# The router of a mixture-of-experts layer taken earlier in the attention trunk, in five units instead of four

## The reference

```python
x = x + xattn0(ctx, layernorm(x), ctx)     # 16 heads of 64, causal
x = x + ffn0(layernorm(x))                 # fp4 quantised, inner width 352
x = x + xattn1(layernorm(x), ctx)          # 16 heads, keys in two segments (77 and 51)
x = x + moe(layernorm(x))                  # 8 experts, the best 2 of each token

def moe(x):                                # x: 2048 tokens x 128
    logits = silu(x @ rw1 + rb1) @ rw2 + rb2            # 128 -> 512 -> 8
    k_logits, k_index = top_k(logits, 2); k_prob = softmax(k_logits)
    out = 0
    for e in range(8):
        we = sum(where(k_index == e, k_prob, 0), -1)
        out = out + we[:, None] * (silu(x @ w1[e] + b1[e]) @ w2[e] + b2[e])   # 128 -> 512 -> 128
    return out
```

## Time and profile before

| | us |
|---|---|
| median of 3 runs | 739.5 |
| the profiled execution | 740.57 |
| its span, first to last instruction | 738.8 |
| PE busy in the span | 644.8 (87%) |
| DVE busy | 534.2 (72%) |
| ACT busy | 437.4 (59%) |
| POOL busy | 305.8 (41%) |

### The profile page before, as it was taken

The page is one execution under the profiler, slowest core; times in us unless marked ns, Lnnn a source line. Parts: engine busy times, 40 slices in busy tenths (PEclk is TensorE's granted clock), DMA queues, the critical chain, the costliest instruction groups (busy, mean ns, idle before and its releaser), DMA issues.

```text
span 738.8 us, 16537 instructions
## 1 busy us (share of the span) xinstructions
PE 644.8 (87%) x5835; PEld 588.2 (80%) x5835; DVE 534.2 (72%) x1444; ACT 437.4 (59%) x1117; POOL 305.8 (41%) x427
## 2 busy tenths in 40 slices
PE   2789999999989989999999999999999539866990
PEld 2678888888878889999999999998887539866990
DVE  7796586888888889888988968776666244533554
ACT  3568878787777765555655555567365107323760
POOL 3234344344434532534443424243364454266560
PEclk9789999999999999999999999999999659867996
DMA  9600000000000002177550500000000011111225
GB/s 230 200 1 1 3 1 1 2 1 1 3 1 1 3 15 69 48 142 129 110 108 1 144 2 2 1 1 3 1 26 19 16 38 50 37 41 51 66 55 177
DMA packets 49390, 33.27 MB, mean 45 GB/s; under 512 B 9415, under 2 KB 45869, under 8 KB 49309
## 3 DMA queue, kind: packets, MB, share of 16 engines
q1 hardware_dynamic: 47036, 27.55, 15.8%
q0 software_dynamic: 2272, 4.67, 1.9%
HBM read 17.57 MB, written 14.63 MB: 44 GB/s over the span
## 4 chain that ended last, share of the span: by engine, by line
PE 53%; DVE 15%; issue 13%; ACT 8%; POOL 5%; DMA 4%; SPq 1%; POOLq 0%; DVEq 0%; ACTq 0%
PE ps_j L386 7%; PE ps_s L535 6%; PE ps_h L610 5%; PE ps_t L574 5%; PE ps_h L589 5%; ACT scores L727 4%; PE ph L1390 4%; PE ps_j L348 4%; DVE scores L989 4%; PE py L1404 4%; PE ps_j L350 3%; PE ps_j L349 3%; DVE neg_max L996 3%; POOL xs_scratch L1318 2%; PE pf L498 2%
## 5 line engine op out<-in xcount | busy, mean ns | idle before, releaser
L1230 POOL TENSOR_TENSOR probs<-scores,rsums 128x308 f32<-128x308 f32 (+1 forms) x192 | 151.9, 805 | 228.9 <-DVE rsums L1009 228.7
L1004 DVE TENSOR_REDUCE sums<-scores 128x4 f32<-128x308 f32 (+1 forms) x192 | 90.9, 501 | 43.8 <-ACT scores L727 34.6
L574 PE MATMUL ps_t<-ident,probs 128*128 128x128 f32 x512 | 79.3, 278 | 17.5 <-ACT probsT L739 17.2
L727 ACT ACTIVATE scores<-scores,neg_max 128x128 f32<-128x128 f32 x256 | 81.6, 393 | 17.5 <-DVE neg_max L996 17.0
L739 ACT ACTIVATE probsT<-ps_t 128x512 f32<-128x512 f32 x128 | 75.4, 589 | 23.8 <-PE ps_t L574 23.8
L634 ACT ACTIVATE QT<-ps_j 128x512 f32<-128x512 f32 x64 | 38.2, 598 | 80.5 <-PE ps_j L350 80.4
L535 PE MATMUL ps_s<-KT,QT 64*128 64x128 f32 x1024 | 77.1, 292 | 0.8 <-ACT KT L640 0.8
L574 PEld LDWEIGHTS ps_t<-ident,probs 128*128 128x128 f32 x512 | 58.9, 143 | 23.3 <-issue 21.5
L589 PE MATMUL ps_h<-probsT,V 128*64 128x128 f32 x1024 | 71.4, 282 | 0.8 <-DVE x_sb L775 0.8
L535 PEld LDWEIGHTS ps_s<-KT,QT 64*128 64x128 f32 x1024 | 64.6, 194 | 9.1 <-issue 1.9
L610 PE MATMUL ps_h<-Wo,headsT 128*128 128x128 f32 x512 | 71.1, 283 | 0.2 <-ACT headsT L745 0.2
(11 more groups left out here) (236 smaller groups left out, 1620.0 us busy)
## 6 DMA issues: line engine op xcount, KB each, us to landing
xs_scratch<-xs SPq DMA_DIRECT2D x8, 1032.0 KB, 8.1
xt<-xs_scratch SPq DMA_DIRECT2D x39, 64.5 KB
w1b<-in_L_ffn_w_dram SPq DMA_DIRECT2D x1, 2048.0 KB, 9.6
big_raw<-in_L_ffn_w_dram SPq DMA_DIRECT2D x8, 256.0 KB, 4.4
ysum<-y_scratch SPq DMA_DIRECT2D x4, 512.0 KB, 5.3
x_sb<-in_x_dram SPq DMA_DIRECT2D x4, 256.0 KB, 3.6
ctx_sb<-in_ctx_dram SPq DMA_DIRECT2D x4, 256.0 KB, 4.9
Wo<-in_L_xattn_Wo_dram SPq DMA_DIRECT2D x2, 512.0 KB, 6.7
```

Source lines behind the costliest of these rows:

```text
L574: ins = nc.tensor.transpose(ps_pT[:, j * S:(j + 1) * S], probs[s % 2][:, j, :], ident[:, :])
L727: ins = nc.scalar.activation(scores[s % 4][:, j, :], scores[s % 4][:, j, :], ACT.Exp, bias=neg_max[:, s % 4, 0, j:j + 1])
L1004: ins = nc.vector.tensor_reduce(sums[:, p4, i, :], scores[p4][:, :, k0:k1], AX_X, ALU.add)
L1230: ins = nc.gpsimd.tensor_tensor(probs[(s - 1) % 2][:, :, k0:k1], scores[r][:, :, k0:k1], rsums[:, r, i, :].rearrange("p (h a) -> p h a", a ...
```

## The change

Units replace quads: `UNITS` is (0,4), (4,4), (8,4), (12,2), (14,2) in batches. Units 0, 1 and 2 start at steps 114, 117 and 120 instead of 116, 121 and 126, so that two units are in progress at a time; their list is made at step 124 instead of 131. Unit 3 (batches 12, 13) is routed in steps 128 to 131, with the tail's own silu. Unit 4 (batches 14, 15) is handled between tiles 0 and 10. The norm slots of the pairs start at other steps, pairs 3, 4, 5 and 6 earlier. The bias transposes go to step 98. Each `router_up` of units 0 to 2 now takes one bank (`pf[0]`) in four turns, half of them at the end of the step; the logits take `pf[1]`, and the totals for the list are a fourth piece of `ranks`. The sends stand at steps 118 to 127 (three in a step, then two); those of unit 3 follow the trunk. The last two trunk steps are woven with the start of the tiles: `turn(0)` stands after step 130, in bank `py[0]`, and DVE copies tile 0's weights before step 130. `late_list` is cut in three: `early_done` (tile 3), `late_tiles` (7), `late_list` (9). `RING` is 8, and there are 6 buffers `ysb`.

```diff
-RING = 6
+UNITS = [(0, QUAD), (QUAD, QUAD), (2 * QUAD, QUAD), (3 * QUAD, PAIR), (3 * QUAD + PAIR, PAIR)]
+RING = 8
+YB = 6
...
-            q, t = divmod(N - FFN_TO, 5)
-            return (q, t) if 0 <= q < EARLY_Q else (None, None)
+        D_AT = [(81, 83, 84, 85), (91, 93, 94, 95), (101, 103, 104, 105), (106, 107, 108, 109), (111, 112, 113, 114),
+                (116, 117, 118, 119), (124, 125, 126, 127), (NG * STEPS + 4,)]
+        BIAS_AT = 98
+        ROUTE_FROM = (114, 117, 120, NG * STEPS)
+        LIST_AT = ROUTE_FROM[EARLY_U - 1] + 4
+        TAIL = NG * STEPS + 2
...
+            def route_end(u, t):
+                if u < EARLY_U:
+                    if t < 2:
+                        router_up(u, 2 * t + 1)
+                    if t == 2:
+                        router_logits(u)
+                    if t == 3:
+                        ranks(u, u == EARLY_U - 1)
+                else:
+                    if t == 0:
+                        router_up(u, 2)
+                        router_up(u, 3)
+                    if t == 1:
+                        router_logits(u)
+                    if t == 2:
+                        ranks(u, False)
...
+            TWIN_AT = (110, 113, 119, 127)
+            SEND_AT = [{118: range(0, 3), 119: range(3, 6), 120: range(6, 8)},
+                       {121: range(0, 3), 122: range(3, 6), 123: range(6, 8)},
+                       {124: range(0, 2), 125: range(2, 4), 126: range(4, 6), 127: range(6, 8)}]
...
+            tail(TAIL)
             turn(0)
+            tail(TAIL + 1)
+            tail(TAIL + 2)
...
+            for N in range(TAIL, TAIL + 3):
+                tail(N)
+            for j in range(TOPK):
+                send(U - 1, 0, j)
             rstd_of(GROUPS - 1, 2, "D")
-            twin(Q)
+            for j in range(TOPK):
+                send(U - 1, 1, j)
+            twin(U)
             for i in range(NT):
-                if 11 <= i < 11 + QUAD:
-                    for j in range(TOPK):
-                        send(Q, i - 11, j)
+                if 7 <= i < 7 + PAIR * TOPK:
+                    send(U, (i - 7) // TOPK, (i - 7) % TOPK)
                 scatter(i)
...
             sp.wait_ge(MS["list"], 1)
-            sp.wait_ge(s_sent, 16 * TOPK * EARLY_Q * QUAD)
+            sp.wait_ge(s_sent, 16 * EARLY_ROWS // P)
```

More of the change, by code:

```diff
@@ L515, in step @@
+            def step(G, g, s, lay, prev, first=False, last=False, nxt=None, f=None, fd=None):
                 n = G * STEPS + s
@@ L625, in trunk_tensor @@
             pe.wait_ge(s_split0_lo, 3)
-            trunk(pe, step)
-            return turn_d, router_up, router_logits, ranks, totals
+            return trunk(pe, step), turn_d, router_up, router_logits, ranks
         def trunk_scalar(act):
@@ L762, in trunk_scalar @@
             copy_k(0, 0)
-            trunk(act, step)
-            return mean_square, high
+            return trunk(act, step), mean_square, high, router_silu
         def trunk_vector(dve):
@@ L1019, in shifted_scores, with step @@
                 ins.then_inc(SS["shifted"], 1)
-            def step(G, g, s, lay, prev, first=False, last=False, nxt=None, f=None):
+            def step(G, g, s, lay, prev, first=False, last=False, nxt=None, f=None, fd=None):
                 n = G * STEPS + s
@@ L1217, in slot, with step @@
                     rstd_of(c, 1, "C")
-                if s == 6 and d is not None:
-                    rstd_of(d, 2, "D")
-            def step(G, g, s, lay, prev, first=False, last=False, nxt=None, f=None):
+            def step(G, g, s, lay, prev, first=False, last=False, nxt=None, f=None, fd=None):
                 n = G * STEPS + s
@@ L1458, in moe_gpsimd @@
         def moe_gpsimd(pool, pieces):
-            rstd_of, twin, send = pieces
-            Q = QUADS - 1
+            tail, rstd_of, twin, send = pieces
+            U = len(UNITS) - 1
             def scatter(i):
@@ L1481, in moe_vector @@
         def moe_vector(dve, pieces):
-            slot, choose, place, late_list = pieces
+            tail, slot, choose, place, early_done, late_tiles, late_list = pieces
             chain = Chain(dve, "m_chain")
-            Q = QUADS - 1
+            U = len(UNITS) - 1
             def gate_difference():
@@ L1545, in moe_vector @@
             stage_w2(0, e)
+            for N in range(TAIL, TAIL + 3):
+                tail(N)
+            for part in (1, 2):
+                slot(5, part, d=GROUPS - 1)
             for i in range(NT):
```

501 lines of the change are left out of this document (259 added, 242 removed).

## The result

The changed kernel took 710.65 us (median of 4 runs, 708.93 to 714.26), the kernel before 739.98 beside it (738.93 to 741.65). The ratio is 0.9608, 95% interval 0.9562 to 0.9654: 29 us faster. The forecast was 700 in a range of 688 to 715. The time lies in the forecast's range; the gain is 29 us where 40 were forecast. Where a run took over 1.5% more than the fastest of its kernel, its ratio is over the other runs (experiment 2 alone has one).

A forecast was written before the change was run, and what follows sets the result against it. PE bounds the trunk; about 35 us lie in two gaps behind it. Stretches of 495.3, 81.3, 15.5, 41.4, 43.5 and 22.1 end at 699.1; plus 1.8, less 1.1 gives 699.8, called 700, range 688 to 715.

The forecast's parts named there:

- The first gap: From 570.0 to tile 0's first matmul at 609.4: early sends, landing and load leave the path; 39.4 us becomes 15.5.
- The tail: Step 128's transposes to tile 0: 8.3 us of PE work, 12 with waits, 3.5 for half clock, sum 15.5 us.
- Tiles 0 to 15: Tiles 31.2, unit 4's PE pieces 5.9, waits 1.0, 1.5 and 1.8: sum 41.4 us instead of 61.0.
- a closed second gap: In tiles 0 to 15: four late sends from tile 7, not eight from 11, and a split list; 61.0 becomes 41.4.
- Tiles 16 to 38 and the end: Later tiles take 43.5 us instead of 46.3 with more buffers; scatter, reading back and weighted sum stay 22.1.
- Steps 114 to 127: Last trunk steps gain 6.6 us: logits 3.6, ranks 0.9, half clock 1.7, totals and transpose 0.4; 74.7 becomes 81.3.
- 49 us in about 58, it fits: POOL in steps 118 to 127: 24 sends 30.5, probabilities 12.5, copies and roots some 6, within the time available.
- 1.7 us each: Trunk's last steps: each group of logits is followed by 3.4 us at clock 0.50, so the third brings 1.7 too.
- the finer weave: `router_up` of units 0 to 2 in one bank, four turns: costed at nothing, up to 1 us a turn if ACT is late.
- The rule and the rows: Skill's rule, clock closes on idleness, would make the sum 3.4 us lower; the forecast followed the trace's rows instead.
- a step 128 beyond 585 would say that the denser trunk isn't only the sum of its matmuls: Warning sign at the end of the trunk's last steps; step 128's transposes were forecast at 576.6.
- the rivals: Tail stays long 0.17; second gap half closes 0.12; even better 0.17; slower 0.02; change doesn't do what it says 0.02.

The follow-up runs named there:

- experiment 2: Changed kernel with the logits of units 0 to 2 in two groups of 16, a turn apart; 706.51 us, ratio 0.9512 to the kernel before.
- experiment 1: Changed kernel with all 24 early sends moved behind step 132 on POOL; 737.35 us (one run).
- the kernel after: The changed kernel itself, with the whole change against the kernel before; 710.65 us, ratio 0.9608.
- Experiment 7: Changed kernel with unit 4's ranks, placing, list parts and late sends one tile later; 712.22 us, ratio 0.9616 to the kernel before.
- experiment 10: Changed kernel with unit 4's pieces back at their earlier places between the tiles, sends at tiles 11 and 12; 712.41 us, ratio 0.962 to the kernel before.
- Experiment 4: Changed kernel with 6 buffers xt and 4 buffers ysb as before, instead of 8 and 6; 715.65 us, ratio 0.9656 to the kernel before.
- experiment 11: Kernel of experiment 9 with norm slots of pairs 3 and 4 partly later and gate values behind the last tile; 704.93 us, ratio 0.9512.
- experiment 5: Changed kernel with logits of units 0 to 2 summed over only 128 of 512 hidden values; 698.12 us, ratio 0.9441 to the kernel before.
- experiment 6: Changed kernel with units 0 to 2 starting at steps 114, 118, 122, list at step 126, later sends; 720.6 us, ratio 0.972 to the kernel before.
- experiment 9: Changed kernel with logits of units 0 to 2 turned round, router weights stationary and hidden values moving; 705.16 us, ratio 0.9537 to the kernel before.
- experiment 8: Changed kernel with norm slots of pairs 3 and 4 one step later in part; 709.3 us, ratio 0.9586 to the kernel before.
- experiments 3: Changed kernel with tile 0's turn, copy and weights behind the last trunk step, not woven in; 714.32 us, ratio 0.9652 to the kernel before.

## Why the forecast was right, and where it was short

**The first gap: right.** The tail was sized 4.7 us too long: 3.5 of them are the half clock, for it ran at 1.00 throughout (and half of 8.3 us of work would have cost 4.2, not 3.5), the rest are waits. The mechanism, early sends that leave only x itself on the path, is shown by experiment 1: 27.3 us come back when they go.

**Tiles 0 to 15: right, 3.2 us short, all of it waits.** PE's busy time, 36.9, is the forecast's 31.2 + 5.9. The waits are 7.7 instead of 4.3: 2.5 for `chosen`, 1.1 for `w1s`, and the rest where a part of the list stands on DVE in front of the next weights. DVE's timeline of the kernel after (answers to the earlier trace rows):

```profile
622.25 0.28 DVE L1233 TENSOR_TENSOR over<-pf,iota_m 128x128 f32<-128x128 f32 x1
...
623.60 0.17 DVE L1238 TENSOR_TENSOR tiles_e<-done_e,tiles_e 128x8 f32<-128x8 f32 x1
624.54 0.43 DVE L1558 COPY w1s<-w1b 128x516 f32 x1 [0.78 <-DVE tiles_e L1238]
```

Here one part of the list takes 1.5 us, and 0.8 pass until the engine takes the copy up, with PE's weights for `ph` waiting until 625.04. I had cut the list into parts and priced each against DVE's slack, without the gap behind each. Experiment 7 shows that moving such a piece only moves its cost. That no `px` waits over 1 us for `xt` was right. Of the two reasons that the forecast gave for a closed second gap, half as many late sends and an earlier start for them, the earlier start alone turned out to be worth little (experiment 10).

**Tiles 16 to 38 and the end: right** (44.1 for 43.5, 22.3 for 22.1). Experiment 4 gives the rings 2.2 us there; the 0.6 that the sum was short, and more, are the gate values in tile 18 (1.5 us, experiment 11), a piece of DVE that it did not name.

**Steps 114 to 127: the step that failed**, 88.0 for 81.3. The work term was right to 0.2 us, and so was POOL: "49 us in about 58, it fits", with sends of 1.04 us; experiment 1 takes them away and the stretch stays. (A send and its issue were added up as 1.26, though 1.03 and 0.3 are 1.33; nothing hangs on it.) Two terms were too small. The first is the half clock, "1.7 us each" for three groups: 8.5 us instead of 5.1 in this execution. The mechanism was the one that the forecast read from the earlier trace rows, that the clock falls behind a group of logits; experiment 5 shows it by its absence. Its size was the mistake: before, both groups were followed by 3.4 us, and I took that as the price of a group. In the profiles here the same three groups bring 13.6 to 27.3 us in 14 steps, and the rows say what goes with the length. In steps 114 to 127 of the profiles with whole groups of 32 pairs, the kernel before among them, the fall came 11 times behind the start of the group's last matmul, and every time the piece at 0.50 was 3.4 us long; both groups of the earlier trace rows are of this kind. It came 15 times inside a group, so that the rest of the logits ran at half clock, and 14 of those pieces were 6.8 to 13.7 us long (one was 3.4). In the kernel after, units 0 and 1 are of the first kind and unit 2 of the second: 1.7 + 1.7 + 5.1 is the 8.5. What decides where in a group the fall comes is not shown; a pitch of four steps did not make it better (experiment 6), and experiment 2 leaves open whether a split does. The second is the waits, 5.5 us for 2.0. I had costed the finer weave at nothing, with up to 1 us for each turn as its price if it was late; PE's waits name `hidT`, `xnT_lo` and `probs` with 4.5 us together. Taking the sends away leaves 3.8, so up to 1.7 us are POOL's; that the rest is the router's own chain in shorter turns fits the names of the waits and was not tried.

**The rule and the rows.** In the kernel after PE is busy 3.76 of 3.80 us ahead of the first fall and all the time behind it, and no wait of it in these steps is longer than 1.6 us. The Trainium skill, page "TensorE: Matmul & The Clock Gate", "Part 1: The HAM clock gate", has the clock close on idleness. By that rule steps 114 to 127 would have had none of the 8.5 us; the rows disagree, and experiment 5 says that they had them because of the logits. What these have of their own is the form: 32 pairs that load 128 x 128 weights to move 8 columns. Turned round (experiment 9) the same sums leave 6.8 us at 0.50, and none in experiment 11. No fall in either profile comes inside a group of turned logits or within 6 us behind it.

**Ahead of step 114**, 2.4 us were lost and none forecast: the forecast left the stretch up to step 114 as it was, although the change moves pieces of PE into it. The rows at experiment 8 show 1.45 us of work, 0.75 of waits and 0.2 from before step 98.

**In sum**: + 2.4 ahead, + 6.7 in the trunk, - 4.7 in the tail, + 3.2 and + 0.6 in the tiles, + 0.2 at the end, 8.4 us on 699.1. The forecast's own mark, "a step 128 beyond 585 would say that the denser trunk isn't only the sum of its matmuls", was met at 585.7. Of the rivals none is what happened: the tail is short and the second gap closed.

## What to carry to other kernels

A chain of waits that names an engine is a question: take that engine's work away from the stretch (experiment 1) before it is called the bound. Split a stretch into work, clock and waits, since kernels compared by their sum alone differ by a clock that varies more than most edits. Do not take the price of a slow piece from two cases that were alike: look at where in the work the clock fell. And on an engine that is full, matmuls that load wide weights for a few moving columns cost more than their own time; turning the operands round, though it adds a copy and transposes, won 5.5 us here.

## What the runs showed of the hardware

The granted clock fell to 0.50 (1.2 GHz) inside or straight behind groups of narrow matmuls, with PE busy throughout each piece at 0.50 in steps 114 to 127 of the kernels with narrow logits: for 3.4 us each time that the fall came behind the group, for 6.8 to 13.7 us in 14 of the 15 times that it came inside; 13.6 to 27.3 us in all over the same 14 steps. With a quarter of those matmuls it did not fall there once. Runs of the kernels with turned logits lie within 0.5%, those of the kernel after within 0.8%, of the one with the logits in two halves within 1.8%; but those of experiments 3 and 7, narrow logits too, lie within 0.4%, so the spread does not follow the form.
